# A fused low-rank feed-forward kernel: low-rank tile products of 32x64 over pairs of batch rows, in place of 32x32 over single ones

## The reference, cut to what matters

```python
# layer 0: gated feed-forward, F = 1376, low-rank terms of rank 16 chosen per batch row
gate = x @ W_gate.T + 0.5 * (x @ A_gate[id].T) @ B_gate[id].T
up   = x @ W_up.T   + 0.5 * (x @ A_up[id].T)   @ B_up[id].T
act  = silu(gate) * up
down = act @ W_down.T + 0.5 * (act @ A_down[id].T) @ B_down[id].T
x    = x + down @ sign(weight).T + bias0
# layer 1: per-row low-rank product, then a dense layer with 8 shared adapters
c    = (x @ B1[id1].T) @ A1[id1].T
x    = x + c @ W1.T + bias1 + sum_n lora_n(c)
```

## Time and profile before

| what | value |
|---|---|
| median of three runs | 920.88 us (920.71 to 922.14) |
| profiled execution, own time | 921.35 us |
| its span, first to last instruction | 919.5 us |
| TensorE matmul busy | 910.7 us, 99% of the span |
| TensorE weight load busy | 723.2 us, 79% |
| VectorE, ScalarE, GpSimd busy | 413.6, 201.1, 105.0 us |

### The profile page before, as it was taken

One profiled execution on the slowest core, in us unless ns is written; L12 is line 12 of the kernel. 1 busy time (PEld: TensorE's weight loads), 2 busy tenths in 40 slices (PEclk: granted clock), 3 DMA queues, 4 the chain that ended last, 5 costly groups with the idle time before them and its releaser, 6 DMA issues.

```text
span 919.5 us, 27778 instructions
## 1 busy us (share of the span) xinstructions
PE 910.7 (99%) x10518; PEld 723.2 (79%) x10518; DVE 413.6 (45%) x1021; ACT 201.1 (22%) x349; POOL 105.0 (11%) x81
## 2 busy tenths in 40 slices
PE   9999999999999999999999999999999999999998
PEld 5887778777887777778778777887777778778775
DVE  5753444444353444434444444353444434444443
ACT  6742112212111111111212212111111111212110
POOL 0210111010111110101111010111110101111011
PEclk9999999999999999999999999999999999999999
DMA  9925454555555455545444544555455545444533
GB/s 340 415 88 138 112 143 134 147 138 133 145 139 138 126 142 147 139 129 149 131 137 136 147 139 135 143 138 139 125 143 147 140 129 150 128 138 137 147 97 90
DMA packets 146839, 134.69 MB, mean 146 GB/s; under 512 B 53249, under 2 KB 118529, under 8 KB 146689
## 3 DMA queue, kind: packets, MB, share of 16 engines
q1 hardware_dynamic: 91152, 108.42, 40.8%
q10 hardware_dynamic: 54720, 22.83, 9.7%
q0 software_dynamic: 944, 3.15, 0.9%
HBM read 92.11 MB, written 11.01 MB: 112 GB/s over the span
## 4 chain that ended last, share of the span: by engine, by line
PE 96%; DMA 1%; DVE 1%; ACTq 1%; issue 1%; SPq 0%; ACT 0%
PE gu_ps L771 54%; PE y_ps L808 25%; PE gu_ps L898 4%; PE out_ps L828 3%; PE out_ps L866 2%; PE y_ps L771 1%; PE out_ps L817 1%; PE out_ps L771 1%; PE out_ps L838 1%; PE gu_ps L890 1%; PE gu_ps L808 1%; DMA weff_raw<-in_w1T 1%; ACTq L248 1%; PE gu_ps L924 0%; DMA landed<-act_sb 0%
## 5 line engine op out<-in xcount | busy, mean ns | idle before, releaser
L771 PE MATMUL gu_ps<-wu_sb,xT_sb 128*128 128x512 f32 (+1 forms) x1152 | 261.1, 371 | 0.3 <-DMA landed<-act_sb 0.3
L771 PE MATMUL gu_ps<-wg_sb,xT_sb 128*128 128x512 f32 (+1 forms) x1152 | 251.9, 367 | 0.1
L808 PE MATMUL y_ps<-down_sb,actT_sb 128*128 128x512 f32 x1023 | 241.1, 393 | 0.0
L808 PEld LDWEIGHTS y_ps<-down_sb,actT_sb 128*128 128x128 f32 x1023 | 189.6, 188 | 64.4 <-issue 26.0
L771 PEld LDWEIGHTS gu_ps<-wg_sb,xT_sb 128*128 128x128 f32 x1152 | 206.8, 188 | 31.4 <-DVE xT_sb L576 1.0
L771 PEld LDWEIGHTS gu_ps<-wu_sb,xT_sb 128*128 128x128 f32 x1152 | 204.4, 188 | 29.6 <-issue 0.7
L576 DVE TENSOR_TENSOR actT_sb<-landed,actT_sb 128x512 fp32r<-128x512 f32 (+1 forms) x96 | 60.7, 633 | 203.9 <-ACT actT_sb L431 203.9
L431 ACT CAST actT_sb<-landed 128x512 fp32r<-128x512 f32 (+1 forms) x96 | 55.9, 585 | 311.9 <-issue 277.9
L396 POOL TENSOR_TENSOR x_in<-x_in,bias_sb 128x512 f32<-128x512 f32 x32 | 41.3, 1291 | 580.5 <-DMA x_in<-in_x 580.5
L617 DVE STREAM_TRANSPOSE lhs_sb<-t_own 32x32 f32<-32x32 f32 x512 | 103.9, 203 | 7.7
L576 DVE TENSOR_TENSOR xT_sb<-xT_raw,xT_sb 128x512 fp32r<-128x512 f32 x32 | 22.1, 691 | 127.0 <-ACT xT_sb L431 127.0
(11 more groups left out here) (135 smaller groups left out, 496.5 us busy)
## 6 DMA issues: line engine op xcount, KB each, us to landing
b_rows<-in_btab SPq DMA_DIRECT2D x128, 216.0 KB
a_raw<-in_atab SPq DMA_DIRECT2D x128, 152.0 KB, 2.3
xT_raw<-in_xT SPq DMA_DIRECT2D x32, 256.0 KB, 2.6
landed<-act_sb ACTq DMA_DIRECT2D x128, 64.0 KB, 2.2
landed<-act_sb SPq DMA_DIRECT2D x128, 64.0 KB, 2.1
x_in<-in_x SPq DMA_DIRECT2D x32, 256.0 KB, 2.8
x_landed<-x_turn ACTq DMA_DIRECT2D x124, 64.0 KB, 2.2
out_x<-out_sb SPq DMA_DIRECT2D x31, 256.0 KB, 2.9
```

The source lines that it names most:

```text
L771: last = nc.tensor.matmul(o, w, m, start=start and n == 0, stop=stop and n == len(terms) - 1, skip_group_check=not check)
L808: last = nc.tensor.matmul(to[:], actT_sb[:, ACTT_SLOT[c] + n, a, :], down_sb[:, blk, b, :], start=begin and (c, n) == (0, 0) and (a, b) == ...
```

## The change

Pairs of batch rows share a tile. The transposed coefficients of batch row b = 2n stay on the even partitions of a row group, and those of b = 2n+1 now go to the odd ones: the constant row gets a second slot and a mask by the token's batch row parity, and `scale_small` writes both slots (64 coefficients become 128 elements, one of the two zero). So `lhs_sb[group(r), pair(n)]` is 32x64 and block-diagonal in the interleaved sense. The loads put the rows of b on partitions of parity b % 2 in slot b // 2, so `b_rows` and `cs_rows` have half the slots and no zeros are needed: both GpSimd zeroings, VectorE's zeroing of `t_own` and the `rows_clear` semaphore go, and the SyncE queue itself waits for what GpSimd waited for. `first_rows` and `second_rows` loop over two pairs in place of four rows: 8 tile products of 32x64 each in place of 16 of 32x32. `second_rows` goes by pair and then by row group 0 to 3. The same holds for the `out_rows` and `down_rows` in `finish`. 8 KB a partition are left unused where the halved buffers were.

```diff
-    scale = np.full((P, SMALL), LORA0_SCALE, np.float32)
+    scale = np.full((P, SMALL, 2), LORA0_SCALE, np.float32)
     scale[:, T1_AT:] = 1.0
+    scale *= (p[:, None, None] // SEQ % 2 == np.arange(2)).astype(np.float32)
...
-        b_rows = place("b_rows", [P, GB, PAIR], f32)
-        cs_rows = place("cs_rows", [P, GB, H], f32)
+        b_rows = place("b_rows", [P, PAIRS, PAIR], f32)
+        cs_rows = place("cs_rows", [P, PAIRS, H], f32)
...
+        cursor[0] += 8192
         loop_end = cursor[0]
...
-        def even_rows(r0, r1):
-            return slice(r0 * QUAD, r1 * QUAD, 2)
+        def rows_of(b, r0, r1):
+            return slice(r0 * QUAD + b % 2, r1 * QUAD, 2), b // 2
+        def pair(n):
+            return slice(n * 2 * SEQ, (n + 1) * 2 * SEQ)
...
-                    sp.dma_start(b_rows[even_rows(0, 4), b, :],
+                    rows, n = rows_of(b, 0, 4)
+                    sp.dma_start(b_rows[rows, n, :],
...
-            sp.wait_ge(S["rows_clear"], 1)
+            sp.wait_ge(S["sbd_mm"], 2)
+            rows_stored(sp)
             load_b(0)
-            sp.wait_ge(S["rows_clear"], 2)
+            sp.wait_ge(S["down_mm"], NBLK)
...
-            pool.wait_ge(S["sbd_mm"], 2)
-            rows_stored(pool)
-            nc.gpsimd.memset(b_rows[:], 0.0).then_inc(S["rows_clear"], 1)
             pool.dma_start(bias_sb[:], bias).then_inc(S["bias_in"], 16)
-            pool.wait_ge(S["down_mm"], NBLK)
-            nc.gpsimd.memset(cs_rows[:], 0.0).then_inc(S["rows_clear"], 1)
...
-                nc.vector.tensor_tensor(t_own[:, c0:c1, 0], small_ps[:, c0:c1], small_scale[:, c0:c1], ALU.mult
+                nc.vector.tensor_tensor(t_own[:, c0:c1, :], small_ps[:, c0:c1].unsqueeze(2).to_broadcast([P, c1 - c0, 2]),
+                                        small_scale[:, c0:c1, :], ALU.mult).then_inc(L["small_scaled"], 1)
...
-            nc.vector.memset(t_own[:], 0.0).then_inc(S["zeroed"], 1)
-            dve.wait_ge(S["zeroed"], 2)
+            dve.wait_ge(S["zeroed"], 1)
...
-            def out_rows(b, r=2):
-                return nc.tensor.matmul(out_ps[tokens(b), :], lhs_sb[group(r), tokens(b)], cs_rows[group(r), b, :],
+            def out_rows(n, r=2):
+                return nc.tensor.matmul(out_ps[pair(n), :], lhs_sb[group(r), pair(n)], cs_rows[group(r), n, :],
                                         start=True, stop=True, skip_group_check=True)
...
             def second_rows():
-                for b, r in [(b, r) for rows in ((2, 3), (0, 1)) for b in range(GB) for r in rows]:
-                    c, u = 1 + r // 2, r % 2
+                for n in range(PAIRS):
+                    for r in range(4):
+                        c, u = 1 + r // 2, r % 2
```

More of the change, by code:

```diff
@@ L67, in constants @@
     ident = np.eye(P, dtype=np.float32)
-    scale = np.full((P, SMALL), LORA0_SCALE, np.float32)
+    scale = np.full((P, SMALL, 2), LORA0_SCALE, np.float32)
     scale[:, T1_AT:] = 1.0
-    return np.concatenate([ident, scale, p[:, None].astype(np.float32)], axis=1).astype(np.float32)
-CONST_W = P + SMALL + 1
+    scale *= (p[:, None, None] // SEQ % 2 == np.arange(2)).astype(np.float32)
+    return np.concatenate([ident, scale.reshape(P, 2 * SMALL), p[:, None].astype(np.float32)], axis=1).astype(np.float32)
+CONST_W = P + 2 * SMALL + 1
+PAIRS = GB // 2
 def build_adaln_ffn(nc, xT, x, wgu, signT, wd, bd, btab, atab, la, lbw, w1T, a1, b1tab, b1end,
@@ L128, in build_adaln_ffn @@
         ident = const_sb[:, 0:P]
-        small_scale = const_sb[:, P:P + SMALL]
-        row_number = const_sb[:, P + SMALL:CONST_W]
+        small_scale = const_sb[:, P:P + 2 * SMALL].rearrange("p (c e) -> p c e", e=2)
+        row_number = const_sb[:, P + 2 * SMALL:CONST_W]
         def in_place(name, shape, at):
@@ L183, in build_adaln_ffn @@
                  "weff_hi", "weff_lo", "a1_hi", "a1_lo", "c_mm", "c_out", "wg_hi", "wg_lo", "wu_hi", "wu_lo",
-                 "silu_ready", "zeroed", "rows_clear")
+                 "silu_ready", "zeroed")
         S = {n: sem("pro_" + n) for n in names}
@@ L321, in load_sbd @@
                     at = row_of(0, g, b, R0)
-                    sp.dma_start(cs_rows[even_rows(3, 4), b, :], sb_view[bass.ds(at, P), :].rearrange("(r e) w -> r (e w)", e=8)
+                    rows, n = rows_of(b, 3, 4)
+                    sp.dma_start(cs_rows[rows, n, :], sb_view[bass.ds(at, P), :].rearrange("(r e) w -> r (e w)", e=8)
                                  ).then_inc(L["sbd_in"], 16)
@@ L327, in load_c @@
                     at = row_of(1, g, b, R1)
-                    sp.dma_start(cs_rows[even_rows(to, to + 1), b, :], c_view[bass.ds(at, P), :].rearrange("(r e) w -> r (e w)", e=8)
+                    rows, n = rows_of(b, to, to + 1)
+                    sp.dma_start(cs_rows[rows, n, :], c_view[bass.ds(at, P), :].rearrange("(r e) w -> r (e w)", e=8)
                                  ).then_inc(signal, 16)
@@ L607, in scale_small @@
                 dve.wait_ge(L["small_mm"], g + 1)
-                nc.vector.tensor_tensor(t_own[:, c0:c1, 0], small_ps[:, c0:c1], small_scale[:, c0:c1], ALU.mult
-                                        ).then_inc(L["small_scaled"], 1)
+                nc.vector.tensor_tensor(t_own[:, c0:c1, :], small_ps[:, c0:c1].unsqueeze(2).to_broadcast([P, c1 - c0, 2]),
+                                        small_scale[:, c0:c1, :], ALU.mult).then_inc(L["small_scaled"], 1)
             def turn_small(g, rows, group_of=range(4), signal=L["lhs_ready"]):
@@ L863, in small, with down_rows @@
                 last.then_inc(L["small_mm"], 1)
-            def out_rows(b, r=2):
-                return nc.tensor.matmul(out_ps[tokens(b), :], lhs_sb[group(r), tokens(b)], cs_rows[group(r), b, :],
+            def out_rows(n, r=2):
+                return nc.tensor.matmul(out_ps[pair(n), :], lhs_sb[group(r), pair(n)], cs_rows[group(r), n, :],
                                         start=True, stop=True, skip_group_check=True)
-            def down_rows(b, to=y_ps, begin=True):
-                return nc.tensor.matmul(to[tokens(b), :], lhs_sb[group(3), tokens(b)], cs_rows[group(3), b, :],
+            def down_rows(n, to=y_ps, begin=True):
+                return nc.tensor.matmul(to[pair(n), :], lhs_sb[group(3), pair(n)], cs_rows[group(3), n, :],
                                         start=begin, stop=False, skip_group_check=True)
@@ L883, in first_rows @@
                 w = CHUNKS[0][1]
-                for b in range(GB):
+                for n in range(PAIRS):
                     if pp is not None:
-                        out_rows(b)
+                        out_rows(n)
                     if prev is not None:
-                        down_rows(b)
+                        down_rows(n)
                     for u in range(2):
-                        last = nc.tensor.matmul(gu_ps[GU_BANK[0][u]][tokens(b), 0:w], lhs_sb[group(u), tokens(b)],
-                                                b_rows[group(u), b, 0:w], start=False, stop=True, skip_group_check=True)
+                        last = nc.tensor.matmul(gu_ps[GU_BANK[0][u]][pair(n), 0:w], lhs_sb[group(u), pair(n)],
+                                                b_rows[group(u), n, 0:w], start=False, stop=True, skip_group_check=True)
                 last.then_inc(L["first_mm"], 1)
             def second_rows():
-                for b, r in [(b, r) for rows in ((2, 3), (0, 1)) for b in range(GB) for r in rows]:
-                    c, u = 1 + r // 2, r % 2
[L897 to L900, removed]
+                for n in range(PAIRS):
+                    for r in range(4):
+                        c, u = 1 + r // 2, r % 2
+                        lhs = lhs_sb if c == 1 else lhs2_sb
+                        last = nc.tensor.matmul(gu_ps[GU_BANK[c][u]][pair(n), :], lhs[group(r), pair(n)],
+                                                b_rows[group(r), n, CHUNKS[0][1]:PAIR], start=False, stop=True,
+                                                skip_group_check=True)
                 last.then_inc(L["second_mm"], 1)
@@ L941, in finish @@
                 pe.wait_ge(L["c_in"], 16 * GB * g)
-                for b in range(GB):
-                    last = down_rows(b, y_end, False)
+                for n in range(PAIRS):
+                    last = down_rows(n, y_end, False)
                 last.then_inc(L["y_mm"], 1)
-                for b in range(GB):
-                    last = out_rows(b)
+                for n in range(PAIRS):
+                    last = out_rows(n)
                 last.then_inc(L["first_mm"], 1)
@@ L964, in finish @@
                 keep_busy(1)
-                for b in range(GB):
-                    last = out_rows(b, 1)
+                for n in range(PAIRS):
+                    last = out_rows(n, 1)
                 last.then_inc(L["first_mm"], 1)
```

## The result

The changed kernel takes 910.55 us (median of four runs, 909.71 to 911.25), the kernel before, run beside it, 921.51 us (four runs, 920.71 to 923.16). The ratio is 0.9878 with a 95% interval of 0.986 to 0.9897: 1.2% faster. The forecast was 909.2 us, or 11.7 us less than before; measured are 11.0 us less by the medians and 11.6 us by the spans of the two profiled executions (919.5 and 907.9).

A forecast was written before the change was run, and what follows sets the result against it. The prediction took TensorE's own work to bound the kernel. 0.38 us saved in each of 31 steps gave 11.8 us, less 0.03 and 0.05, so 11.7 off 920.88: 909.2 us, range 907.3 to 914.

The forecast's parts named there:

- The bound: Whole kernel: TensorE, busy 99% of the span, sets the time, so shortening its work shortens the step.
- The halt: Second block's loads: a 0.19 us gap from at most 64 TensorE instructions under way, gone with 64 a step.
- Rivals 2 and 3: Second block still halts 0.19 us, 917.5 us, chance 0.10; only tile stagger saved, 919.4 or 918.9 us, chance 0.03.
- Four passes and the switch: Row group 3's path in a step: 4 x 0.43 = 1.72 us streaming, then 0.09 us switching back to 128x128.
- a 64-column load: Tile weight load in the low-rank products: 28 ns more than a 32-column load, bounds 0 and 85 ns.
- Rival 4: Low-rank blocks: two 64-column tiles of one row group take turns, 1.72 us more a step, 962 us, chance 0.05.
- Rival 1: Second block: products still enter 0.017 us apart, saving 0.31 a step, 911.3 us (up to 913.2), chance 0.08.
- step 1: Loop step without `out_rows`: same four passes and halt on row group 3, so counted alike at 0.38 us.
- Step 0: First loop step: gains nothing, because its next gate waits for `act_done` of the first chunk.
- `scale_small`: ScalarE's coefficient copy: 0.07 us longer, covered by 1.9 us of slack in the loop; 0.05 us more in `finish`.
- The prologue: Before the loop: first `b_rows` loads go at about 44 rather than 47.18, but TensorE has no gap, so 0.

The follow-up runs named there:

- 17 against 18 products: The changed kernel with one or two 352-column products of the first block cut in two, same columns: 909.89 us with one cut, 915.97 us with two.
- 32x32 with 64 instructions: The kernel before with low-rank products of only two of the four batch rows, so its result is not the reference's: 910.33 us in one execution.
- a first product of 352 columns: The kernel before with first_rows issuing all eight 352-column products ahead of the eight of 512 columns: 918.91 us, ratio 0.9972.
- with 20: The changed kernel with all four 352-column products of the first block cut in two, 80 instructions: 915.01 us in one execution.

## Why the prediction was right

- **The bound.** TensorE's own work shortened the step by the same amount: the products of a step take 0.39 us less, and the mean step of the loop is 0.38 us shorter (26.52 to 26.14). No other engine's work came in between.
- **The halt is a count of instructions, not a tile.** Shown from four sides: 17 against 18 products (a jump of 0.204 us between them, with the last product's load 0.03 us after the oldest is finished), 32x32 with 64 instructions (1.86 us), a first product of 352 columns (the halt ends at 0.80 in place of 1.07), and the new order alone (no gain). Rivals 2 and 3 of the prediction fell with the first profile, 1.89 against the 2.17 and more that they needed. One thing stays open: every product here is two loads and two matmuls in turn, so no run can tell a limit of 64 instructions from one of 32 matmuls or of 32 loads. It is not a limit of 16 whole products, since in the kernel before a seventeenth gets its first load at 411.77, 0.6 us before the first has finished.
- **The terms.** Four passes and the switch were right; a 64-column load takes 132 ns against 103 for 32 columns, 29 ns more where 28 were taken from the neighbours. The sum was 1.90 us and the trace has 1.89. Rival 4 (tiles of one row group take turns) would have needed 3.6.
- **Rival 1**, the slow feed of 0.017 us, exists only behind a halt: with 16 products the second block's loads follow their tiles; with 20 the three products behind the halt come 0.017 us apart.
- **Steps and covers.** The products of 30 steps gave 0.389 us each and those of step 1 gave 0.336 (2.211 to 1.875, where 0.38 was counted), 12.0 us together, against 11.8. Step 0 gave 0.01. `scale_small` went from 225 to 292 ns, as worked out, and no wait follows it. The prologue is worth 0, by experiment.
- **What the sum left out.** The products gave 12.0 us and the spans 11.6. Outside the pattern both executions have a handful of idle times of TensorE that are not the same ones: before, 1.91 and 0.94 us labelled "issue" ahead of line 838 and 0.52 ahead of the last `down`; after, 0.62 "issue", 1.00 ahead of the last `down`, 1.56 and 0.27 in the tail. They add up to 3.36 and 3.45 us. That these nearly cancel was luck for the forecast: it had treated nearly everything outside the products as unmoved. They account for 0.1 us of the 0.4 between products and spans; the rest is not explained. The tail's part is explained (the SyncE queue works through its loads one after another, and TensorE gained on it: the last x load is issued 4.8 us ahead of the last `down_rows` before, 3.3 us after) and was removed. Where the 1.91 us of the kernel before comes from stays open, but it is hardly chance: at the same place it is 1.95 us in the kernel with only the new order and 1.38 us with the narrow products first, and no kernel with 16 to 20 products has it there; these have one "issue" of 0.3 to 2.0 us a step later. So which of them a kernel has goes with its program, and the forecast had no term for it.

## What to carry to other kernels

In this kernel small tile products side by side are bounded by two things that the busy share does not show: the columns each tile streams, and how many instructions are under way. Count the load and matmul instructions from the oldest product still streaming to the one wanted next, and if there are more than 64, make each product wider, or put the short ones first so that the oldest ends early. When a bracket says "issue", look for an earlier instruction whose end stands 0.03 us ahead of the resumption, and check the guess in a step of the same kernel that has fewer instructions.

## What the runs showed of the hardware that was not expected

- Below the limit, wide and narrow f32 tiles cost the same per pass: 512 columns keep a tile 0.43 us whether it is 32x32 or 32x64, and 352 columns 0.30 us. A product of 16 columns on a tile that has to stream 336 more cost 0.007 us (17 products, 1.896 us for 1.889).
- Matmuls do not start in program order across row groups. In the rows of the kernel after, the second passes of the 352-column products (line 895) start from 0.36 us, and that of the first `out_rows` (line 871), which stands ahead of them in the program, at 0.48. In the single records of a middle step of the kernel after, likewise, pair 1's second-block products on row groups 0 and 1 start at 0.68 us, and pair 0's on row groups 2 and 3, which stand ahead of them in the program, at 0.91 (the records do not name a row group; it is read from when its tile is free). The Trainium skill, "TensorE: Matmul & The Clock Gate", section "The mechanism", says that matmuls start and end strictly in program order; for the starts the trace does not agree, and the measurement decides; the ends are modelled, so they show nothing here.
- With the halt gone, a step has no idle weight-load time labelled "issue" between the blocks, yet PE's busy share did not change from 99%.
